# Both digit scans of a recurrent step from one strided table of fifteen places per batch

## The reference

```python
def step(carry, xs):
    h, c = carry
    i_t = sigmoid(xi_t + h @ V_i); f_t = sigmoid(xf_t + h @ V_f)
    g_t = tanh(xg_t + h @ V_c);    o_t = sigmoid(xo_t + h @ V_o)
    c_new = h * c + i_t * g_t
    h_new = o_t * tanh(c_new)
    return (h_new, c_new), h_new
```

## Time and profile before

| | |
|---|---|
| median of 3 runs | 4079.02 us (4078.55 to 4084.59) |
| profiled execution | 4080.13 us, span 4078.4 us |
| busy, share of the span | PE 89%, DVE 84%, ACT 65%, POOL 53%, PEld 65% |
| steps of the recurrence | 3136 |

### The profile page before, as it was taken

The page is one execution under the profiler, slowest core; times in us unless marked ns, Lnnn a source line. Parts: engine busy times, 40 slices in busy tenths (PEclk is TensorE's granted clock), DMA queues, the critical chain, the costliest instruction groups (busy, mean ns, idle before and its releaser), DMA issues.

```text
span 4078.4 us, 134734 instructions
## 1 busy us (share of the span) xinstructions
PE 3620.0 (89%) x35548; PEld 2656.5 (65%) x35548; DVE 3425.5 (84%) x21828; ACT 2635.9 (65%) x11666; POOL 2154.5 (53%) x3173
## 2 busy tenths in 40 slices
PE   6799998989898989899999999898989898988887
PEld 5666666666666666666666666666666666666665
DVE  6788888888888888888888888888888888887777
ACT  3366666666666666666666666666666666666665
POOL 6555555555555556555555555555555555652222
PEclk8855555555555555555555555555555555555555
DMA  5000000000000000000000000000000000000000
GB/s 73 2 1 1 1 1 1 1 1 1 1 1 1 1 1 1 1 1 1 1 1 1 1 1 1 1 1 1 1 1 1 1 1 1 1 2 1 1 1 1
DMA packets 44538, 11.08 MB, mean 3 GB/s; under 512 B 39913, under 2 KB 44010, under 8 KB 44490
## 3 DMA queue, kind: packets, MB, share of 16 engines
q1 hardware_dynamic: 42378, 10.05, 1.7%
q10 hardware_dynamic: 2112, 0.46, 0.1%
HBM read 7.29 MB, written 3.21 MB: 3 GB/s over the span
## 4 chain that ended last, share of the span: by engine, by line
PE 57%; ACT 18%; DVE 18%; issue 6%; POOL 1%; DMA 0%; ACTq 0%; DVEq 0%; POOLq 0%
PE GATES L1267 12%; ACT O L698 10%; PE GATES L1284 9%; PE YB L1087 9%; ACT G L695 8%; DVE HR L917 8%; DVE O L914 8%; PE TAPB L1074 6%; PE YB L1238 6%; PE DB L1206 5%; PE DB L1068 3%; PE H1B L1114 1%; PE H2B L1114 1%; PE H2B L1062 1%; PE TAPB L1121 1%
## 5 line engine op out<-in xcount | busy, mean ns | idle before, releaser
L695 ACT ACTIVATE G<-GATES 128x12 f32<-128x12 f32 x3136 | 573.4, 183 | 1197.8 <-PE GATES L1284 1149.3
L1267 PE MATMUL GATES<-HR,VN 128*128 128x4 f16 x3136 | 536.3, 171 | 357.5 <-DVE HR L917 239.3
L1284 PEld LDWEIGHTS GATES<-HR,VN 128*128 128x128 f16 x6272 | 423.0, 107 | 657.7 <-issue 593.4
L909 DVE TENSOR_TENSOR_SCAN CT<-G,CT 128x12 f32<-128x12 f32 x3136 | 586.7, 187 | 272.1 <-ACT G L695 250.6
L698 ACT ACTIVATE O<-G 128x16 f32<-128x16 f32 x3136 | 690.5, 220 | 99.2 <-ACT G L695 0.2
L914 DVE RECIPROCAL O<-O 128x4 f32<-128x4 f32 x3136 | 567.6, 181 | 198.7 <-ACT O L698 1.0
L1280 PEld LDWEIGHTS <-VN 128*128 128x128 f16 x3136 | 457.6, 146 | 345.8 <-issue 309.5
L917 DVE TENSOR_TENSOR_SCAN HR<-O,CT 128x20 f16<-128x20 f32 x3136 | 613.4, 196 | 5.2
L1284 PE MATMUL GATES<-HR,VN 128*128 128x4 f16 x6272 | 617.1, 169 | 0.0
L1284 PE MATMUL GATES<-H,VW 128*128 128x4 f16 x6272 | 615.7, 169 | 0.0
L926 DVE SCALAR_TENSOR_TENSOR CT<-HIST,CT 128x4 f32<-128x4 f32 x3136 | 523.7, 167 | 108.8
(11 more groups left out here) (242 smaller groups left out, 7023.1 us busy)
## 6 DMA issues: line engine op xcount, KB each, us to landing
out_dram<-OUT SPq DMA_DIRECT2D x112, 28.0 KB, 2.0
X<-in_x_dram SPq DMA_DIRECT2D x4, 672.0 KB, 11.5
STG<-in_L_ffn_w_dram SPq DMA_DIRECT2D x4, 512.0 KB, 12.6
U<-in_L_conv_U2s_dram SPq DMA_DIRECT2D x1, 972.0 KB
W<-in_L_ffn_w_dram SPq DMA_DIRECT2D x1, 512.0 KB, 11.9
X<-in_x_dram ACTq DMA_DIRECT2D x4, 112.0 KB, 3.1
S<-in_L_conv_S1s_dram SPq DMA_DIRECT2D x1, 108.0 KB
S<-in_L_conv_S2s_dram SPq DMA_DIRECT2D x1, 108.0 KB
```

Source lines behind the costliest of these rows:

```text
L695: act.activation(G6[:, :, 2:5], gates[c][:, w, :, :], ACT.Tanh, scale=1 / GSCALE).then_inc(step_in, 1)
L909: dve.tensor_tensor_scan(CELL.rearrange("z b k -> z (b k)"), G6[:, :, :].rearrange("z b k -> z (b k)")[:, 0::2], ADD3.rearrange("z b k -> ...
L1267: return pe.add_instruction(mybir.InstMatmult(name=nc.get_next_instruction_name(), engine=mybir.EngineType.PE, start_tensor_calc=False, st ...
L1284: last = pe.matmul(gates[c][:, w, :, SLOT[g]], wt[:, g].rearrange("z m c -> z (m c)"), digit, start=False, stop=True, skip_group_check=True)
```

## The change

O5 with its two halves becomes one table OD with 15 places for each sequence, and TC5 becomes TD, also with 15. The first scan reads every fifth place of both (0, 5, 10: three for each sequence, 12 elements), the second every third (0, 3, 6, 9, 12: still 20). So o is written to the places 3, 5, 12 and 14 (16 values as before; 14 is read by none), T to 0 and 9, the reciprocal from place 3 to place 9. The constants lie at 6 and 10 (-1) and 3, 6, 5, 10 (GRID). HR shrinks to 3 places for each sequence. At setup more floats are cleared, and one constant is set in two instructions instead of one.

```diff
-        O5 = sb("O5", [128, 2, B, 5])
-        HR = sb("HR", [128, B, 5], F16)
+        OD = sb("OD", [128, B, DP15])
+        HR = sb("HR", [128, B, 3], F16)
...
-        TC5 = CT[:, 32:52].rearrange("z (b k) -> z b k", k=5)
+        TD = CT[:, 32:32 + B * DP15].rearrange("z (b k) -> z b k", k=DP15)
...
+        def places_of_o():
+            a = OD[:, :, 3]
+            return bass.AP(a.tensor, a.offset, [a.ap[0], [DP15, B], [2, 2], [9, 2]])
...
-                    act.activation(O5[:, :, :, 1:5:3], G6[:, :, 3:4].unsqueeze(1).broadcast_to([128, 2, B, 2]), ACT.Copy, scale=O_MAX, bias=1.0)\
+                    act.activation(places_of_o(), G6[:, :, 3:4].unsqueeze(2).broadcast_to([128, B, 2, 2]), ACT.Copy, scale=O_MAX, bias=1.0)\
...
-                    act.activation(TC5[:, :, 0:4:3], CELL[:, :, 2:3].broadcast_to([128, B, 2]), ACT.Tanh, scale=0.5)\
+                    act.activation(TD[:, :, 0:10:9], CELL[:, :, 2:3].broadcast_to([128, B, 2]), ACT.Tanh, scale=0.5)\
...
-                    dve.reciprocal(O5[:, 1, :, 3], O5[:, 1, :, 1]).then_inc(rec_done, 1)
+                    dve.reciprocal(OD[:, :, 9], OD[:, :, 3]).then_inc(rec_done, 1)
...
-                    dve.tensor_tensor_scan(HR[:, :, :].rearrange("z b k -> z (b k)"), O5[:, 0].rearrange("z b k -> z (b k)"),
-                                           TC5.rearrange("z b k -> z (b k)"), 0.0, op0=ALU.mult, op1=ALU.add)\
+                    dve.tensor_tensor_scan(HR[:, :, :].rearrange("z b k -> z (b k)"), OD[:, :, :].rearrange("z b k -> z (b k)")[:, 0::5],
+                                           TD.rearrange("z b k -> z (b k)")[:, 0::5], 0.0, op0=ALU.mult, op1=ALU.add)\
...
-                    dve.tensor_tensor_scan(H5[:, :, :].rearrange("z b k -> z (b k)"), O5[:, 1].rearrange("z b k -> z (b k)"),
-                                           TC5.rearrange("z b k -> z (b k)"), 0.0, op0=ALU.mult, op1=ALU.add)\
+                    dve.tensor_tensor_scan(H5[:, :, :].rearrange("z b k -> z (b k)"), OD[:, :, :].rearrange("z b k -> z (b k)")[:, 0::3],
+                                           TD.rearrange("z b k -> z (b k)")[:, 0::3], 0.0, op0=ALU.mult, op1=ALU.add)\
...
-                    dve.tensor_tensor(HIST[:, t, :], O5[:, 0, :, 1], TC5[:, :, 0], ALU.mult).then_inc(h_done, 1)
+                    dve.tensor_tensor(HIST[:, t, :], OD[:, :, 5], TD[:, :, 0], ALU.mult).then_inc(h_done, 1)
...
-            link(dve, dve.memset(CT[:, 0:52], 0.0))
+            link(dve, dve.memset(CT[:, 0:32 + B * DP15], 0.0))
             link(dve, dve.memset(ADD3[:, :, 0:2], 1.0))
-            dve.memset(TC5[:, :, 1:3], GRID).then_inc(set_dve, 2)
+            link(dve, dve.memset(TD[:, :, 3:7:3], GRID))
+            dve.memset(TD[:, :, 5:11:5], GRID).then_inc(set_dve, 2)
```

More of the change, by code:

```diff
@@ L39 @@
 FIRST = LEAD + 4
+DP15 = 15
 EG = 2
@@ L943, in dve_head_row @@
                     if t == CONST_AT:
-                        for tile_, v in ((HIST, 0.0), (G6, 0.0), (O5, 0.0), (HR, 0.0), (H5, 0.0), (BX, 0.0), (ONEH, 1.0), (WC, 0.0)):
+                        for tile_, v in ((HIST, 0.0), (G6, 0.0), (OD, 0.0), (HR, 0.0), (H5, 0.0), (BX, 0.0), (ONEH, 1.0), (WC, 0.0)):
                             link(dve, dve.memset(tile_[:], v))
-                        link(dve, dve.memset(O5[:, :, :, 2:3], -1.0))
+                        link(dve, dve.memset(OD[:, :, 6:11:4], -1.0))
                     if t == IDUP_AT:
```

## The result

The kernel after takes 4069.85 us (median of 8 runs, 4067.39 to 4070.81), the kernel before on the same chip 4080.33 us (8 runs): a ratio of 0.9972 [0.9962, 0.9983]. By the medians it is faster by 10.5 us, 0.26%. The forecast was 4047 us with a range of 4034 to 4066, so the sign held and the size is a third of what was forecast. A later set on another chip, with 11 runs of after and 15 of before, gave 4068.47 against 4074.47, 0.9983 [0.9974, 0.9992]: 6.0 us.

The account below looks back on a forecast made before the run. The bound was taken to be a loop through TensorE, ScalarE and VectorE, no single engine. Savings of 27.5 us in fifty rows and 4.3 in the last six, less 0.2 for setup, made 31.6: 4047 us, range 4034 to 4066.

Parts of the forecast that it names:

- An element of a scan costs two VectorE cycles, 2.08 ns: First scan HR, 20 to 12 elements: 8 x 2.08 = 16.6 ns off its duration.
- The rival with one cycle: First scan HR: an element costs one cycle, 8.3 ns, half the gain, about 4063 us; chance 0.14.
- The rival that the distance does not shrink: HR to H: H arrives when it did, so the earlier first digit gains nothing, 4079 us; chance 0.10.
- H keeps its 20 elements and its duration.: Second digit scan H: starts 16.6 ns earlier and still takes 171 ns.
- the term of -26.6 us: 32 places per row counted as gaining 16.6 ns each, over the fifty rows with the involution.
- Strides are free: Scans reading every fifth or third float of SBUF and PSUM: no added time.
- The rival "strides cost more": Both scans: each element read a cycle dearer, HR 4.1 ns shorter, H 20.8 longer, 4120 us; chance 0.10.
- A longer O goes nearly whole into the step: ScalarE's O copy: T starts within 0.01 us of its end; no growth was taken, 0.22 us as now.
- (a): Places with products already late, t = 2, 10, 26, 31, 36, 41, 46: nothing gained in these 7.
- (b): Places t = 25, 30, ... before five late ones, where TensorE's filler waits for the PA copy: 5 more gain nothing.
- (c): Six pairs: places 14, 19, ..., 39, where DB and a conv product meet, and those before: 3 ns per pair, not 33.
- The rival that they come back: Late and paired places: if the pairs are not held, 49 places of a row gain, 46 us, 4033 us; chance 0.10.

Follow-up runs that it names:

- dense_short: Kernel before with dense tables, only the first scan cut from 20 to 12 elements (wrong digits); 4057.41 us against 4073.43, 0.9956.
- dense_four: Kernel before with dense tables, only the first scan cut from 20 to 4 elements (wrong digits); 4043.05 us beside 4071.93.
- after_hr3: Kernel after with its first scan reading 12 elements at every third float instead of every fifth (wrong digits); 4055.67 us beside 4075.67.
- s5p3_short: Kernel before with places five floats apart in SBUF, three in PSUM, first scan cut to 12 elements; 4070.57 us beside 4080.2.
- s3p5_short: Kernel before with places three floats apart in SBUF, five in PSUM, first scan cut to 12 elements; 4053.39 us beside 4080.2.
- after_w3first: Kernel after with TensorE's expert product issued ahead of the taps product that waits for the PA copy; 4051.33 us beside 4075.67, 0.9941.
- psum3: Kernel before with only the PSUM table spread to every third float, both scans keeping 20 elements; 4076.64 us beside 4073.43.
- convfirst: Kernel after with the conv product issued ahead of DB at t = 14, 19, ..., 39; 4080.93 us beside 4080.2, 1.0003.
- after_best: Kernel after with expert product ahead of taps, conv product of t = 2 at 3, conv ahead of DB except at t = 19; 4051.62 us beside 4074.47.
- after_again: Kernel after unchanged, measured once more on another chip; 4068.47 us against 4074.47 for the kernel before.
- both3: Kernel before with the tables in SBUF and PSUM spread to every third float, both scans keeping 20 elements; 4079.39 us beside 4073.43.
- before_w3first: Kernel before with TensorE's expert product issued ahead of the taps product that waits for the PA copy; 4059.01 us beside 4075.67, 0.9957.

## Why the prediction was wrong, point by point

- **A loop through three engines, and T releases HR.** Right. T's end to HR is 32 to 33 ns in every kernel, and G to the start of HR 629 to 632.
- **An element of a scan costs two VectorE cycles, 2.08 ns.** Right. HR takes 196, 179 and 162 ns with 20, 12 and 4 elements, 16 to 17 ns for 8. The rival with one cycle (4063 us) came nearer to the time, but for a wrong reason. The Trainium skill's statement in DVE: opcode table, instruction layouts, handler registers and perf-mode slots, section 6, that the scan runs at half rate, agrees with these rows.
- **H starts earlier by the same.** Right: HR to H 112 to 95 ns. The rival that the distance does not shrink falls.
- **"H keeps its 20 elements and its duration."** This is the step that failed. H grew by 10 ns: 6 because its predecessor is shorter (dense_short, dense_four), 4 because the predecessor reads SBUF at every fifth float (after_hr3, s5p3_short against s3p5_short). Of 16.6 ns 6.3 were left at H's end and 5.3 in the step, and the term of -26.6 us became -8.5. Why an instruction behind a shorter one takes longer no run shows; that it does is shown. The rows of before could have warned: two scans of the same 20 elements took 196 ns (HR, after a wait) and 171 (H, right behind HR), so a duration was not the instruction's own there.
- **Strides are free.** Right for the scans that read them (HR 177 to 179 in all short kernels), for a stride of three in both memories and of five in PSUM. Wrong for a stride of five in SBUF, whose price appears on the instruction behind: 4 ns on H after HR, and perhaps the 9 on HIST where H has that stride (there HIST's own floats also lie 25 apart, not 15 as in after). The evidence I used, HIST with its floats 20 bytes apart, was itself four elements long. The rival "strides cost more" had the right kind, a longer H, for another reason: it charged H's own elements 20.8 ns, and H lost 4 ns to what its predecessor reads, and not in every step (in after_w3first H takes 176 to 178 in 42% of them).
- **The rule of the Trainium skill.** SBUF — State Buffer, "Door 1: The DMA port swizzle" gives four floats as the widest free stride in SBUF; of PSUM, with lines of 8 bytes, it says that non-contiguous access slows matmuls. In SBUF the side on which three and five fall agrees with these runs, though the price came on the instruction behind the reader (H 177 and 181 ns). In PSUM the prediction carried the line size over to VectorE's reads; there strides of three and five floats cost nothing (H 169 in psum3, 177 in s3p5_short), and the measurement decides.
- **A longer O goes nearly whole into the step.** Wrong. O grew by 11 to 12 ns (writes spread over SBUF) and G to HR did not move: T waits for CT and starts 34 ns after its end either way, while O's end went from 2 ns ahead of T's start to 10 behind it, so T does not wait for O at all. "Both sides end together" was read from hundredths of a microsecond; a start that follows an end by 0.01 us is not released by it when every release in the loop takes 0.03 or more.
- **Lost places.** Right, and nearly to the number: -1.0 us for the pairs against -0.9, +0.6 against 0 for (a) and (b). The 3 ns a pair were an allowance and not worked out from a row, so that they came out (3.4) is luck; the mechanism is not: the two steps of a pair of (c) sum to 2448 ns in after, after_hr3, dense_short and dense_four, while a quiet step is 1220, 1214, 1217 and 1208. The rival that they come back (4033 us) falls. That the order of the filler holds them was shown by w3first for (b) and the five late places of (a), and by convfirst for (c) at five of the six. For t = 2 the reason given was not the one: the step became quiet when the conv product left it (1253 to 1217 in after_best).
- **t = 10.** Not foreseen: TensorE comes to the norms' product 42 ns later in 25 of 50 rows of after, in 8 of 50 of after_again, in 22 of both3, and in none of before. It varies between executions of one kernel, and the product's input (RSE, from GpSimd) had been ready for 1.0 us. It costs 0.3 to 1.1 us and stays open.

With the measured 5.3 ns in place of 16.6, the prediction's own count gives 32 x 5.3 x 50 = 8.5, 0.9 for the pairs and 1.4 for the tail: 10.8 us less in the loop, which lost 9.3; the 1.5 between them are t = 10 and the places of (a) and (b). The 8.5 is bookkeeping and no test, since the 5.3 was read from those same places. The sum would be 4069.3 us for the profiled execution, which took 4068.7, and that closeness is luck: 2.2 us of the latter's gain lie before the loop. The range failed because it was built from doubts about HR and from strides on the reader, with no bound for the instruction behind.

## What to carry to other kernels

Price a shortened instruction by when its successor ends, not by its own duration: here the scan behind a shorter scan took longer, and of 16.6 ns saved on the first scan 10 got through, and 6 with the stride of five. Before shortening anything in a loop, list the places where another engine is late; the gain is nil there. Changing the order of the filler, so that no waiting product stands ahead of a ready one, brought more (16.7 us in before_w3first) than the change did (10.5 and 6.0). And of every product that is moved ahead, look up what it waits for itself.

## What the runs showed of the hardware

- VectorE: a 20-element scan takes 171, 177 and 184 ns behind scans of 20, 12 and 4 elements; behind 12 it takes 176 without a wait of its own. The first scan takes 196, 179 and 162 ns with those counts, 2.1 ns an element.
- A scan that reads SBUF at every fifth float makes the next one longer, H from 177 to 181 ns in nearly every step of after and s5p3_short, but only in 58% of the steps of one execution of after_w3first; its own duration stays. At every third float, and in PSUM at either, there is no such cost. HIST, behind an H that reads at every fifth float, takes 142 instead of 133; whether H's stride or its own does that was not told apart.
- ScalarE: 16 values written to scattered places of SBUF take 220 ns in the dense tables of 40 floats and 230 to 231 in those spread by three or five, and with the shared table 232.
- Quiet steps of this loop lie on levels 6.7 ns apart; with 4 ns less in one instruction (after_hr3 against after) the step fell by a level, 1220 to 1213, and the loop by 12.6 us.
- TensorE: a product behind the wait for the copy starts 55 ns after the copy's end at t = 16 and 21 and 129 to 136 ns after it at t = 26 to 46, where a second, long fulfilled wait stands before it.
